# Cross-attention and frequency-domain feed-forward on one core: the keys' inputs first, both key halves ahead of the query fills, and the last six matrix sums on GpSimd

## The reference

```
x = x + xattn(layernorm(x), ctx, mask)        # x: 2 x 2048 x 512, ctx: 2 x 128 x 512
    q, k, v = projections of x, ctx, ctx; 16 heads of 32
    score = q k^T / sqrt(32) * mask; score = where(score == 0, -1e9, score)
    out   = softmax(score) v @ wo + bo
x = x + ffn(layernorm(x))
    real(ifft(fft(x) @ (w_real + i w_imag))) + bias   # one real 512 x 512 matrix M, made once
```

## Time and profile before

| | before |
|---|---|
| median of 3 runs | 457.48 us (457.0 to 458.08) |
| the profiled execution, own time | 456.98 us |
| its span in the trace | 455.2 us |
| busy: PE, DVE, ACT, POOL | 433.3, 403.5, 368.3, 353.0 us |
| granted PE clock, all 40 slices | 9 (90% or more of full speed) |

### The profile page before, as it was taken

One profiled execution on the slowest core, in us unless ns is written; L12 is line 12 of the kernel. 1 busy time (PEld: TensorE's weight loads), 2 busy tenths in 40 slices (PEclk: granted clock), 3 DMA queues, 4 the chain that ended last, 5 costly groups with the idle time before them and its releaser, 6 DMA issues.

```text
span 455.2 us, 10923 instructions
## 1 busy us (share of the span) xinstructions
PE 433.3 (95%) x3510; PEld 298.5 (66%) x3510; DVE 403.5 (89%) x538; ACT 368.3 (81%) x1342; POOL 353.0 (78%) x476
## 2 busy tenths in 40 slices
PE   6989897998999999999999999999999999989997
PEld 5777676777566676666676666666766665555444
DVE  3797699889999999999999999999999899999353
ACT  3358597789998989998989899899989899999620
POOL 6588844685879989798989898989899877755763
PEclk9999999999999999999999999999999999999999
DMA  8996662332426455564555445546443424341244
GB/s 287 389 376 183 234 199 70 93 92 60 107 72 153 109 156 115 141 133 125 117 153 117 132 87 138 128 123 153 108 104 66 109 69 115 55 92 24 71 110 122
DMA packets 85287, 60.15 MB, mean 132 GB/s; under 512 B 40142, under 2 KB 72814, under 8 KB 84719
## 3 DMA queue, kind: packets, MB, share of 16 engines
q1 hardware_dynamic: 84508, 59.29, 48.4%
q10 hardware_dynamic: 722, 0.17, 0.2%
HBM read 29.33 MB, written 8.39 MB: 83 GB/s over the span
## 4 chain that ended last, share of the span: by engine, by line
PE 58%; DVE 14%; POOL 10%; issue 8%; ACT 7%; DMA 1%; ACTq 1%; POOLq 0%; DVEq 0%
PE bank L454 24%; PE bank L459 15%; PE bank L611 7%; ACT zs L714 5%; PE bank L625 4%; DVE zs L904 4%; PE scores L599 3%; DVE zs L897 3%; PE bank L560 2%; POOL cl L1146 2%; POOL rzb L1140 2%; POOL xs L1093 2%; ACT pt L723 1%; PE bank L541 1%; DMA bqb<-in_bq 1%
## 5 line engine op out<-in xcount | busy, mean ns | idle before, releaser
L714 ACT ACTIVATE zs<-zs,nbias 128x128 f32<-128x128 f32 x512 | 199.5, 395 | 18.1 <-POOL nbias L1133 17.3
L714 ACT ACTIVATION_READ_ACCUMULATOR zs<-zs,nbias 128x1 f32 x512 | 98.4, 192 | 0.0
L904 DVE SCALAR_TENSOR_TENSOR zs<-zs 128x1024 f32<-128x1024 f32 x64 | 89.7, 1401 | 1.2
L909 DVE TENSOR_REDUCE nmin<-zs 128x8 f32<-128x1024 f32 x64 | 78.1, 1220 | 2.2
L897 DVE TENSOR_TENSOR zs<-scores,ms 128x1024 f32<-128x1024 f32 x64 | 78.1, 1220 | 1.0 <-issue 0.6
L723 ACT COPY pt<-bank 128x512 f32<-128x512 f32 x128 | 67.8, 580 | 13.5 <-PE bank L611 13.4
L611 PE MATMUL bank<-ident,zs 128*128 128x128 f32 x512 | 66.8, 273 | 1.9 <-ACT zs L714 1.9
L459 PE MATMUL bank<-xth,wqh 128*128 128x256 f16 x224 | 61.2, 273 | 1.3 <-DVE ql L869 1.3
L1093 POOL TENSOR_TENSOR xs<-xs,bob 128x512 f32<-128x512 f32 (+1 forms) x41 | 42.9, 1049 | 25.0 <-DVE zs L904 21.9
L459 PE MATMUL bank<-xtl,wqh 128*128 128x256 f16 x224 | 61.1, 273 | 0.0
L459 PE MATMUL bank<-xth,wql 128*128 128x256 f16 x224 | 61.1, 273 | 0.0
(11 more groups left out here) (126 smaller groups left out, 929.2 us busy)
## 6 DMA issues: line engine op xcount, KB each, us to landing
xs<-in_x SPq DMA_DIRECT2D x16, 512.0 KB, 4.5
xtr<-in_xt SPq DMA_DIRECT2D x16, 512.0 KB, 4.5
out<-x SPq DMA_DIRECT2D x31, 256.0 KB, 2.5
qs<-qh SPq DMA_DIRECT2D x120, 64.0 KB
lp<-in_lparts SPq DMA_DIRECT2D x4, 1024.0 KB, 8.3
qs<-ql SPq DMA_DIRECT2D x60, 64.0 KB
ms<-in_mask SPq DMA_DIRECT2D x16, 128.0 KB, 2.6
wqs<-in_wq SPq DMA_DIRECT2D x2, 512.0 KB, 6.9
```

What stands on the lines that cost most here:

```text
L714: last = act.activation(z, z, ACT.Exp, bias=nbias[:, s % 4, i:i + 1], scale=-NEG, accum_out=zsum[:, s % 4, i:i + 1])
L904: dve.scalar_tensor_tensor(out=z, in0=z, scalar=0.0, in1=z, op0=ALU.is_equal, op1=ALU.subtract).then_inc(eq_done, 1)
L909: dve.tensor_reduce(nmin[:, s % 4, :], zs[:, s % NZ].rearrange("p t h k -> p (t h) k"), AX.X, ALU.min).then_inc(mn_done, 1)
```

## The change

Eight edits, all in the first 110 us of the program. (1) SP loads the identity, the context and both halves of the key weights ahead of the query weights. (2) PE begins with CT, K 0 and K 1, and only then W1 and the queries; the zeros ahead of everything go from 28 to 14. (3) On DVE, ACT and POOL the steps are reordered to match: K 1 and its two `spread_k` move forward, `moments(1)` moves from ahead of the first query back to just ahead of `mask_mul(0)`, and `moments(2)` from ahead of `mask_mul(1)` to behind `least(1)`. (4) Fill Y goes ahead of V 1. (5) ST 3 goes from the end of slot 3 to between V 1 and Z 0. (6) ST 4 goes from slot 10 to slot 9. (7) Sums 6 to 11 go from DVE to GpSimd: 6 to 8 into slot 3 behind `split_lo(3)`, 9 and 10 into slot 4 behind `bias(4)`, 11 behind `stat_cols(4)`. (8) GpSimd does `spread_k(0)` ahead of `scale_mask(0)`, and no longer waits in between.

```diff
-    lead = [("W1", 0), ("CT", 0), ("CT", 1), ("K", 0), ("ST", 0), ("Q", 0, 0), ("Q", 0, 1), ("S", 0),
-            ("W1", 1), ("Q", 0, 2), ("S", 1), ("K", 1), ("Q", 0, 3), ("ST", 1), ("Q", 1, 0), ("S", 2),
+    lead = [("CT", 0), ("CT", 1), ("K", 0), ("K", 1), ("W1", 0), ("ST", 0), ("Q", 0, 0), ("Q", 0, 1), ("S", 0),
+            ("W1", 1), ("Q", 0, 2), ("S", 1), ("Q", 0, 3), ("ST", 1), ("Q", 1, 0), ("S", 2),
...
-        2: [("V", 0), ("ST", 2)], 3: [("V", 1), ("Y", 0), ("Z", 0), ("Z", 1)],
+        2: [("V", 0), ("ST", 2)], 3: [("Y", 0), ("V", 1), ("ST", 3), ("Z", 0), ("Z", 1)],
...
-        late += [("ST", a) for a in range(3, NC) if row_slot(a) == v]
+        late += [("ST", a) for a in range(4, NC) if row_slot(a) == v]
...
-    return {3: 3, 4: 10}.get(c, 4 * c - 9)
+    return 9 if c == 4 else 4 * c - 9
...
-            load_half(wqs, wq, 0, d_wq)
-            load_x(0)
-            load_xt(0)
             sp.dma_start(ident[:], eye).then_inc(d_eye, 16)
             sp.dma_start(cxs[:], ctx_in.rearrange("b k d -> k b d")).then_inc(d_cx, 16)
             load_half(wks, wk, 0, d_wk)
+            load_x(0)
+            load_half(wks, wk, 1, d_wk)
+            load_half(wqs, wq, 0, d_wq)
+            load_xt(0)
+            load_half(wqs, wq, 1, d_wq)
             load_x(1)
             load_mask(0)
-            load_half(wqs, wq, 1, d_wq)
-            load_half(wks, wk, 1, d_wk)
             load_xt(1)
...
-                    pe.wait_ge(l_done if c < 2 else l_hi, 6)
+                    pe.wait_ge(l_done, 6 if c < 2 else 12)
...
-            zeros(28)
+            zeros(14)
...
-                if v in (4, 5):
-                    for n in range(3 * v - 6, 3 * v - 3):
-                        fold(n)
...
             stat_cols(0)
+            spread_k(0)
             scale_mask(0)
-            pool.wait_ge(p_ms, 1)
-            spread_k(0)
+            spread_k(1)
             stat_cols(1)
             split_lo(1)
...
             pool.wait_ge(l_done, 4)
-            spread_k(1)
             bias(1)
...
                 if v == 3:
                     low_o()
+                if v == 4:
+                    fold(9)
+                    fold(10)
...
+                if v == 4:
+                    fold(11)
                 for a in (3, 4):
                     if lo_slot(a) == v:
                         split_lo(a)
+                if v == 3:
+                    fold(6)
+                    fold(7)
+                    fold(8)
```

More of the change, by code:

```diff
@@ L258, in build @@
             sem(n) for n in ("rz_done", "cn_done", "s1_done", "a1_done", "s2_done", "a2_done", "w_lo"))
-        dc_done, wz_lo, l0_done, m_hi, m_lo, b_zero, l2_done, l_hi, o_lo = (sem(n) for n in ("dc_done", "wz_lo", "l0_done", "m_hi", "m_lo", "b_zero", "l2_done", "l_hi", "o_lo"))
+        dc_done, wz_lo, l0_done, m_hi, m_lo, b_zero, l2_done, o_lo = (sem(n) for n in ("dc_done", "wz_lo", "l0_done", "m_hi", "m_lo", "b_zero", "l2_done", "o_lo"))
         p_l1, p_l2, p_zero = (sem(n) for n in ("p_l1", "p_l2", "p_zero"))
@@ L749, in high_q @@
                 act.activation(wqh[:, :, n], wqs[:, :, n], ACT.Identity, scale=SQ).then_inc(w_hi, 1)
+            act.wait_ge(d_eye, 16)
+            act.copy(ident16[:], ident[:]).then_inc(i16_done, 1)
+            hi(at["K", 0])
             high_q(0)
             split_hi(0)
-            act.wait_ge(d_eye, 16)
-            act.copy(ident16[:], ident[:]).then_inc(i16_done, 1)
+            hi(at["K", 1])
             hi(at["W1", 0])
-            hi(at["K", 0])
             hi(at["ST", 0])
+            hi(at["Q", 0, 0])
             high_q(1)
-            hi(at["Q", 0, 0])
             hi(at["Q", 0, 1])
@@ L764, in _ @@
             exps(0, 0)
-            hi(at["K", 1])
             exps(0, 1)
@@ L940, in mean1 @@
                 dve.bn_aggr(ag1[:, c % 2, t, :], st1[:, t, :]).then_inc(a1_done, 1)
[L942 to L953, removed]
             def last_lo2(t):
@@ L991, in _ @@
             dve.memset(bqb[:], 0.0).then_inc(b_zero, 1)
-            low_q(0)
-            moments(0)
-            lo(at["W1", 0])
             lo(at["CT", 0])
             lo(at["CT", 1])
+            moments(0)
+            lo(at["K", 0])
+            low_q(0)
+            spread_k(0)
             split_lo0()
-            moments(1)
-            lo(at["K", 0])
-            spread_k(0)
+            lo(at["K", 1])
+            lo(at["W1", 0])
             lo(at["ST", 0])
             lo(at["Q", 0, 0])
+            low_q(1)
             lo(at["Q", 0, 1])
-            low_q(1)
+            moments(1)
             mask_mul(0)
@@ L1009, in _ @@
             lo(at["Q", 0, 2])
-            moments(2)
+            spread_k(1)
             mask_mul(1)
             zero_to_neg(1)
-            lo(at["K", 1])
-            spread_k(1)
             least(1)
+            moments(2)
             lo(at["Q", 0, 3])
```

## The result

The changed kernel takes 463.01 us (median of 4 runs, 462.41 to 464.76), the kernel before 457.24 in the same session: a ratio of 1.0134 [1.0121, 1.0148], **5.8 us slower**. The profiled execution has a span of 460.7 us (455.2 before) and an own time of 462.49.

What follows compares the result with a forecast made beforehand. PE bounds the kernel from slot 12 on, so only its entry moves: -0.3 us (slots 3 to 6, late front included) and -0.2 (slot 10) on 456.98 give 456.4, 456.9 on the runs' scale; range 455.0 to 459.0, own 456.0 to 457.9.

Steps and rivals of the forecast that it cites:

- The loads and the first rows: Start of the kernel: first query half lands at 11.5 us, both key halves done before 15, `low_q(1)` at 21.1.
- The front ends 1.2 us later: Up to VectorE's release of Q 0 3: it ends 1.2 us later, bounds 0.3 to 2.2, though K 1's wait goes.
- it adds nothing, with no slack: ScalarE's copy of Q 0 3 at 35.3 to 36.2 us, just ahead of VectorE's 36.3, so no added delay.
- VectorE's run from `low_q(1)` to that release: From 21.1 us to the release of Q 0 3: 14.9 us, less 0.9, plus 1.5.
- one unbroken row: VectorE from 13.0 us: steps end to end, Q 0 0's release at 17.9 us, then on to `low_q(1)`.
- The clock: Slower rival: PE idle 3.5 us from near 33.1 to 36.6 falls to 1.2 GHz; some 3 us, 460; chance 0.08.
- Slots 3 to 6: R 0 waits for GpSimd until 62.65, 2.6 us later; 0.7 and 2.2 come back, QQ 3 1 0.3 earlier.
- the last line: End of the sum: 456.4 us profiled, 456.9 on the scale of the runs' median.
- Slot 10: ST 4 one slot earlier avoids its 1.71 us wait for QQ 4 1's release; gain taken as 0.2 us.
- The tenths that the stacked queries' transfer might hold slot 8: Chunk 2's stacked queries, transferred behind QQ 2 1's release, hold slot 8 a few tenths of a microsecond.
- Edits 4, 5 and 7: Slots 3 to 6: Y and ST 3 moves take a 1.25 us wait, 0.7 returning; GpSimd's sums delay R 0.

Runs made afterwards that it cites:

- e_srow: Changed kernel with ScalarE's copies of Q 0 3 and of chunk 1's statistics row ahead of the exponentials of slot 0: 463.42 us, 1.0135.
- e_skgap: Changed kernel with VectorE's `spread_k(1)` moved into its 1.64 us gap ahead of the release of Q 0 0: 462.24 us, 1.011.
- both together: Changed kernel with `spread_k(1)` in VectorE's gap and ScalarE's copies of Q 0 3 and the statistics row ahead of the exponentials: 460.58 us, 1.0079.
- the kernel with 44 matmuls: Changed kernel with 44 matmuls that nobody reads in PE's 4.95 us wait of Q 1 0, nothing else moved: 461.3 us, 1.0094.
- the fastest kernel: Changed kernel's front with five placements mended, and of its late edits only edit 7: 454.97 us, 0.9943 against the kernel before.
- fourth and fifth place: On the changed kernel: GpSimd's `bias(0)` ahead of its first two sums (with three others 458.31 us); VectorE's Q 0 3 release ahead of `zero_to_neg(1)` (all 456.98 us).
- the program with four places: Changed kernel with `moments(1)` and `spread_k(1)` in VectorE's gap, ScalarE's two copies ahead of the exponentials, `bias(0)` ahead of GpSimd's two sums: 458.31 us, 1.0033.
- the sixth place: The fastest kernel with VectorE's release of ST 1 right behind that of Q 0 3, ahead of `zero_to_neg(1)`: 455.72 us, 0.9964.
- five places: The program with four places plus VectorE's release of Q 0 3 ahead of `zero_to_neg(1)`: 456.98 us with all eight edits, 454.97 without edits 4 to 6.
- e_mom1: Changed kernel with `moments(1)` alone moved into VectorE's gap ahead of the release of Q 0 0: 461.12 us, 1.0095.

## Why the prediction was wrong

**The loads and the first rows: right within a microsecond.** The first query half landed at 11.66 us (forecast 11.5). PE began with K 0 at 8.70 and not at 7.3, so its copies on ScalarE ended at 13.20 (11.9) and both key halves at 15.77, not before 15. `low_q(1)` began at 21.80 (21.1), `stat_cols(1)` at 24.93 (24.2), `bias(0)` at 32.72 (31.9 to 32.9).

**"The front ends 1.2 us later": the step that failed**, in three ways. First, it followed VectorE to the release of Q 0 3 and ended there. It put ScalarE's copy of Q 0 3 at 35.3 to 36.2 and said that "it adds nothing, with no slack". But behind that copy on ScalarE stands ST 1's, the row that closes Q 1 0, and behind Q 1 0 stand the scores of slot 2. PE has both ahead of Q 1 1, so they could no longer be done in the shadow of VectorE's wait: e_srow and e_skgap each mended one of the two chains and won nothing or 0.8 us, both together 2.4. I had listed who waits for the copy named in the row, not for the one queued behind it. Second, a size: VectorE's run from `low_q(1)` to that release was taken at some 15.3 us and measured 17.7 (21.80 to 39.50). The 2.4 us too few are in the main `spread_k(1)`, 3.82 where I took 1.30 from a row in which GpSimd did not hold it; smaller terms that I left out, as the release of Q 0 1, which now stands behind `low_q(1)`, and a gap of 0.54 us in the stretch that I called unbroken, nearly cancel. Third, VectorE had a gap of 1.64 us ahead of the release of Q 0 0, while I had everything after 13.0 in one unbroken row; five steps were in a place where they missed it or held another engine.

**The clock.** Its rival stood at 0.08, with the right mechanism and another waiter: PE idle from 31.93 to 36.88, not from 33.1 to 36.6, and 0.50 of the clock behind it. Its price, "some 3 us", is 1.7 by the medians of the kernel with 44 matmuls and 1.2 by its rows. I gave it a low chance because no row of before shows a fall. That says only that no idle time in before was this long. My own forecast had a stall of 3.5 us where the longest was 1.7, so the rows gave no support for the clock staying up either.

**Slots 3 to 6: right in structure and in size.** R 0 waits for `rzb`. It is 6.9 us late and 1.4 of them are its own (forecast 2.6 with 1.2 from the front, the same 1.4). From R 0 to QQ 3 1 it is 14.4 us (forecast 14.6). The three sums took 3.85 (4.75), and the `rzb` copy 1.60 (0.61): the block that I put on the sums fell on the copy. Some sums of this part are off by 0.1, without consequence: `spread(0)` comes out at 61.9 and R 0 at 62.5, and the last line at 457.0, not 456.9.

**Slot 10: wrong sign.** "Between nothing and 1.7, I take 0.2" for edit 6, a gain; alone it loses 1.0. The wait of 1.71 us did go. I looked at the wait that it takes away and not at which bank each fill behind it now gets. The tenths that the stacked queries' transfer might hold slot 8 were 0.82.

**Edits 4, 5 and 7** were weighed together. Alone, 4 and 5 are nothing and 7 gains 1.1. R 0's wait for `rzb`, of which 1.0 comes of VectorE's pass being ahead of the copy, does not show in the time: the fastest kernel has it too. So late edits that look alike are a gain, nothing and a loss, and together nothing, which is also their sum.

**The sum, by the rows of the profiled execution.** The 5.5 us are 1.2 as forecast, 0.7 by which `low_q(1)` was late, 2.4 of VectorE's longer run and 1.2 of the clock. What stays open is the share of each place: the experiments on single places overlap (0.8, nothing, 1.9 and 1.7 us alone, 2.4 for two, 4.7 for four by their medians), and the shares of the fourth and fifth place alone were not measured.

## What to carry to other kernels

When several engines feed one, list for every step that becomes late not only who waits for it but who waits for each step queued behind it. Two chains that are equally late hide each other, and mending one of them measures as nothing. Before a step is moved into a ring of buffers, count again which buffer every later step gets. And price a forecast stall with the clock in mind: look at each execution's own clock, since a median over executions with different clocks mixes the schedule with the clock.

## What the runs showed of the hardware

**The clock falls behind short stalls, and not always.** Behind 4.95 us without a matmul PE was granted 0.50, in the program with four places 0.50 behind 3.31 us; with both edits the window behind a wait of 2.27 has 0.66, with the sixth place that behind 1.96 has 0.79. The length of the last wait does not settle it: with `moments(1)` moved the clock was 1.00 from 35 to 40 us in spite of a wait of 3.22 us, and 0.66 in the next five, behind a second one of 2.47; edit 7 alone has a wait of 1.91 us and all ten executions at 1.000. Nor does the front alone: five places with 1.60 and 0.19 us gave four of four executions at 1.000 without edits 4 to 6, but 7 of 10 at 0.996 with them, and no trace shows where it fell in those. One and the same program has the fall in some executions and not in others; with four places mended that was 2 us at a mean clock of 0.996 and 5 at 0.989. The Trainium skill (TensorE: Matmul & The Clock Gate, HAM oscillation) warns of idle gaps as the cause; the traces agree in kind.

**16-bit copies on VectorE are held by GpSimd.** Four copies of 32x256 f16 took 3.82 us beside GpSimd's `split_lo(1)` and sums (3.50 in e_mom1) and 1.50 in the gap (e_skgap); I had reckoned with this only for passes with two inputs. Beside GpSimd's own 16-bit copies they were not held: 1.30 at 18.05 and 1.32 at 32.37 in the kernel before. With the `rzb` copy a few tenths of a microsecond of order decided which engine was held. The Trainium skill (SBUF — State Buffer, Who interferes with whom) states that copies too can take the shared ports, in a two-port mode, and that the later one blocks fully. The rows agree with it, and this sentence was there to be read.
